# The Nyquist bin of a spectral attention block, with tokens on partitions and with new orders on all engines

## The reference

```python
query = unit_projection(x @ Wq.T + bq)      # F(x)/(|F(x)|+eps), back
keys, values = unit_projection(...), unit_projection(...)
s = jnp.cumsum(bind(keys, values), axis=1)  # along tokens
out = unbind(s, query)
x = x + out
x = x + ffn(layernorm(x))   # 8 trees of depth 7, 255 nodes: silu(logits) of the path's nodes @ W_out.T
```

## Time and profile before

| | |
|---|---|
| median of 3 runs | 1993.65 us |
| profiled execution | 1992.84 us |
| its span, first to last instruction | 1991.0 us |
| mean granted TensorE clock | 0.987 |
| TensorE busy | 1868.4 us (94%) |
| VectorE busy | 1744.3 us (88%) |
| ScalarE busy | 1131.1 us (57%) |
| POOL busy | 945.9 us (48%) |

### The profile page before, as it was taken

How to read it: one execution, slowest core, us unless ns; L and a number is a source line. 1 busy time by engine, 2 the same in 40 slices (tenths; PEclk the granted TensorE clock), 3 DMA queues, 4 the chain that set the end, 5 groups by cost and what they waited for, 6 DMA issues and landing times.

```text
span 1991.0 us, 39541 instructions
## 1 busy us (share of the span) xinstructions
PE 1868.4 (94%) x14360; PEld 1362.3 (68%) x14360; DVE 1744.3 (88%) x2900; ACT 1131.1 (57%) x2150; POOL 945.9 (48%) x744
## 2 busy tenths in 40 slices
PE   8489999999999999999999999999999999999978
PEld 6367766677766667766667776667776666776655
DVE  4988899988899889899988889998889998889983
ACT  5565555566555566555556555556655555655533
POOL 1354454554444554445555445455444555544540
PEclk9699999999999999999999999999999999999998
DMA  8022232222232222223222223222223322222312
GB/s 272 11 75 76 74 95 74 74 84 74 74 95 91 67 79 76 78 84 95 65 83 84 74 74 95 74 74 90 69 74 95 93 65 79 79 76 83 85 54 64
DMA packets 181642, 163.05 MB, mean 82 GB/s; under 512 B 140146, under 2 KB 140658, under 8 KB 181618
## 3 DMA queue, kind: packets, MB, share of 16 engines
q1 hardware_dynamic: 163186, 95.35, 16.6%
q0 software_dynamic: 18432, 67.38, 10.9%
HBM read 95.58 MB, written 16.78 MB: 56 GB/s over the span
## 4 chain that ended last, share of the span: by engine, by line
DVE 57%; issue 16%; PE 9%; POOL 5%; ACT 4%; DMA 2%; DVEq 1%; SPq 1%; POOLq 0%; ACTq 0%
DVE arena L1186 9%; PE bank_l L507 7%; DVE sp_hat L1131 6%; DVE arena L1209 4%; DVE arena L1199 4%; DVE sp_den L1125 3%; DVE dec L1179 3%; DVE xn_pair L1088 2%; DVE sp_cum L1154 2%; DMA arena<-xn_pair 2%; DVE arena L1142 2%; DVE st L1056 2%; DVE sp_den L1123 2%; DVE arena L1145 2%; DVE arena L1110 2%
## 5 line engine op out<-in xcount | busy, mean ns | idle before, releaser
L507 PE MATMUL bank_l<-arena,win_mem 128*128 128x256 f16 x5376 | 625.7, 273 | 27.4 <-DMA arena<-xn_pair 27.4
L542 PE MATMUL bank_l<-wout_mem,arena 128*128 128x512 f16 x2688 | 590.8, 379 | 0.3 <-DVE arena L1186 0.3
L507 PEld LDWEIGHTS bank_l<-arena,win_mem 128*128 128x128 f16 x5376 | 522.0, 98 | 96.5 <-issue 19.1
L477 PE MATMUL bank_p<-arena,wf_hi 128*128 128x256 f16 x3072 | 508.5, 273 | 18.0 <-DMA arena<-xn_pair 9.9
L542 PEld LDWEIGHTS bank_l<-wout_mem,arena 128*128 128x128 f16 x2688 | 263.0, 98 | 304.0 <-DVE arena L1186 0.8
L477 PE MATMUL bank_p<-arena,wf_lo 128*128 128x256 f16 x1536 | 419.3, 273 | 0.0
L935 POOL TENSOR_TENSOR arena<-arena 128x512 f32<-128x512 f32 x96 | 121.7, 1268 | 617.7 <-ACT arena L697 617.7
L477 PEld LDWEIGHTS bank_p<-arena,wf_hi 128*128 128x128 f16 x3072 | 296.1, 98 | 65.1 <-ACT arena L688 16.7
L742 ACT ACTIVATE arena<-bank_l,bias_in,s_logit 128x256 f32<-128x256 f32 x448 | 225.8, 558 | 168.1 <-PE bank_l L517 167.7
L1186 DVE SCALAR_TENSOR_TENSOR arena<-arena,s_act 128x512 f16<-128x512 f32 (+1 forms) x256 | 252.5, 1006 | 39.6 <-ACT arena L752 39.5
L1179 DVE TENSOR_SCALAR dec<-bank_l,thr,off 128x256 bf16<-128x256 f32 x256 | 131.9, 527 | 64.5 <-PE bank_l L507 64.2
(11 more groups left out here) (180 smaller groups left out, 2722.3 us busy)
## 6 DMA issues: line engine op xcount, KB each, us to landing
arena<-in_x SPq DMA_DIRECT2D x32, 512.0 KB, 3.6
arena<-arena SPq DMA_DIRECT2D x32, 512.0 KB, 2.9
out<-arena SPq DMA_DIRECT2D x64, 256.0 KB, 2.1
wout_mem<-in_w_in_t SPq DMA_DIRECT2D x1, 3584.0 KB, 15.1
arena<-in_w_out_t SPq DMA_DIRECT2D x1, 3584.0 KB, 14.1
arena<-xn_pair SPq DMA_TRANSPOSE x128, 2.7
arena<-in_leaf_rows,leaf_row POOLq DMA_INDIRECT x128, 4.9
win_mem<-in_wq SPq DMA_DIRECT2D x1, 1024.0 KB, 8.3
```

Source lines behind the costliest of these rows:

```text
L477: mm = pe.matmul(bank, a, b, start=(n == 0), stop=(n == len(pairs) - 1))
L507: mm = pe.matmul(bank_l[t % 4][:, c * T:(c + 1) * T], a[:, k, w:w + P], x2t[:, :, b, k, :], start=(c == 0 and k == 0 and m == 0), stop=((t ...
L542: mm = pe.matmul(bank_l[j][:, :], a[:, m, tok], w[:, m, :], start=(m == 0 and a is a_hi and w is wout_hi), stop=(m == DENSE - 1 and a is a ...
```

## The change

The Nyquist values of q, k and v leave the rows for token partitions. `nyquist_rows` turns `sp_raw` (96 partitions by 128 tokens) by two float32 products of 3 columns, into unused columns of `bank_i[1]`. ScalarE takes the size of 6 columns there (`nyquist_size`). VectorE works on 6 columns (`nyquist_den`, `nyquist_inverse`, `nyquist_unit`) and 2 columns (`nyquist_bind`). The running sum along the tokens is five float32 products with an upper triangle and a full square of one value (`nyquist_sums`). `nyquist_unbind` adds the carry and multiplies with q, and `nyquist_carry` makes the next carry. The inverse transform loses its one-row products. Instead the residual adds the value where it folds, with a sign by position. For that the stored order of the features puts odd positions ahead of even ones, and the two cosine folds become four of half the width.

The core of the diff:

```diff
+            def nyquist_rows(n):
+                pe.wait_ge(raw_im, 3 * n + 3)
+                if not isinstance(n, int) or n:
+                    pe.wait_ge(x1_ready, J * n)
+                for j in range(J):
+                    mm = pe.matmul(sp_rows[:, j, :], sp_raw[:, j * P:(j + 1) * P], row_of, start=True, stop=True)
+                mm.then_inc(sp_rows_full, 1)
+            def nyquist_sums(n):
+                pe.wait_ge(sp_kv_ready, n + 1)
+                pe.matmul(sp_sums[:, 0:1], upper, sp_kv[:, 0:1], start=True, stop=True)
+                pe.matmul(sp_sums[:, 1:2], upper, sp_kv[:, 1:2], start=True, stop=False)
+                pe.matmul(sp_sums[:, 1:2], full, sp_kv[:, 0:1], start=False, stop=True)
+                pe.matmul(sp_sums[:, 2:3], full, sp_kv[:, 0:1], start=True, stop=False)
+                pe.matmul(sp_sums[:, 2:3], full, sp_kv[:, 1:2], start=False, stop=True).then_inc(sp_sums_full, 1)
...
-                    if c == 0:
-                        pairs += [(sp_z_hi[:, tok], tab_sp[:, :]), (sp_z_lo[:, tok], tab_sp[:, :])]
...
-                act.activation(sp_den[:, :], sp_raw[:, :], ACT.Abs).then_inc(sp_abs_ready, 1)
+            def nyquist_size(n):
+                act.wait_ge(sp_rows_full, n + 1)
+                act.activation(sp_size, sp_rows, ACT.Abs).then_inc(sp_abs_ready, 1)
...
+            def nyquist_den(n):
+                dve.wait_ge(sp_abs_ready, n + 1)
+                dve.tensor_tensor(sp_den[:, :, :], sp_size, eps_sp[:, :, :], ALU.add).then_inc(sp_den_ready, 1)
+            def nyquist_inverse(n):
+                dve.wait_ge(sp_den_ready, n + 1)
+                dve.reciprocal(sp_den[:, :, :], sp_den[:, :, :]).then_inc(sp_inv_ready, 1)
+            def nyquist_unit(n):
+                dve.wait_ge(sp_inv_ready, n + 1)
+                dve.tensor_tensor(sp_hat[:, :, :], sp_rows, sp_den[:, :, :], ALU.mult).then_inc(sp_hat_ready, 1)
+            def nyquist_bind(n):
+                dve.wait_ge(sp_hat_ready, n + 1)
+                dve.tensor_tensor(sp_kv[:, :], sp_hat[:, :, K], sp_hat[:, :, V], ALU.mult).then_inc(sp_kv_ready, 1)
+            def nyquist_unbind(n):
+                dve.wait_ge(sp_sums_full, n + 1)
+                dve.scalar_tensor_tensor(out=sp_z[:, :], in0=sp_sums[:, 0:J], scalar=sp_carry[:, 0:1],
+                                         in1=sp_hat[:, :, Q], op0=ALU.add, op1=ALU.mult).then_inc(sp_z_ready, 1)
...
-                dve.tensor_tensor(cos[:, 0:QI], ce[:, 0:QI], co[:, 0:QI], ALU.add)
-                dve.tensor_tensor(cos[:, QI:], ce[:, 0:QI], co[:, 0:QI], ALU.subtract)
+                dve.wait_ge(sp_z_ready, i + 1)
+                top, odds, evens = sp_z[:, j:j + 1], slice(0, ODDS), slice(ODDS, QI)
+                for part, sign in ((odds, ALU.subtract), (evens, ALU.add)):
+                    up, down = cos[:, part], cos[:, QI + part.start:QI + part.stop]
+                    dve.scalar_tensor_tensor(out=up, in0=ce[:, part], scalar=top, in1=co[:, part], op0=sign, op1=ALU.add)
+                    dve.scalar_tensor_tensor(out=down, in0=ce[:, part], scalar=top, in1=co[:, part], op0=sign,
+                                             op1=ALU.subtract)
```

The orders of the engines in `step`. On ScalarE, after the copies of the odd parts:

```diff
+                act.activation(root_warm[:, :], ln_eps[:, :], ACT.Sqrt)
                 if attn:
                     evac_re(n, Q)
                     evac_im(n, Q)
                     square(n, Q)
+                std(i, mv2, rs2, ln2_mv, ln2_std)
+                if attn:
                     evac_re(n, K)
-                std(i, mv2, rs2, ln2_mv, ln2_std)
-                if attn:
-                    root(n, Q)
...
                     evac_im(n, K)
+                    root(n, Q)
                     square(n, K)
                     evac_re(n, V)
-                    root(n, K)
                     evac_im(n, V)
                     square(n, V)
...
+                    root(n, K)
                     root(n, V)
```

The silus move ahead of the high parts for trees 4 and 5, and `z_high` comes behind the first `leaf_silu`. On POOL:

```diff
                     sum_squares(n, K)
-                    q_unit(n)
                     sum_squares(n, V)
                     add_eps(n, K)
+                    q_unit(n)
+                fetch(i, 1)
+                if attn:
                     bind(n)
                 fetch(i, 0)
                 if attn:
                     unbind(n)
-                fetch(i, 1)
```

More of the change, by code:

```diff
@@ L623, in step @@
[L623 to L637 removed]
+                logits(i, 0, 0)
@@ L1505, in constants @@
     fwd[P, P:HB] = 0.0
[L1506 removed]
+    inside, even, odd = INSIDE, k[:P], k[P:]
     def angles(f, m):
```

309 lines of the change are left out of this document (155 added, 154 removed).

## The result

| | before | changed |
|---|---|---|
| median, 4 runs each | 1992.68 us | 1973.22 us |
| lowest to highest | 1987.29 to 1995.52 | 1970.82 to 1974.94 |
| ratio, 95% interval | | 0.9905 (0.988 to 0.9929) |
| profiled execution, its span | 1992.84, 1991.0 | 1974.17, 1972.3 |

The kernel is faster by 19.5 us, about 1%. The forecast was 47 us. So the direction and the range held, and more than half of the expected gain is missing.

A forecast was written before the change was run, and what follows sets the result against it. TensorE was taken to set the 59.15 us period: minus 2.94 stalls, minus 0.62, plus 1.8, plus 0.4 stall left gives 57.8. That saves 42 us over 31 periods, 47 with the ends: 1946 us, range 1928 to 1978.

The forecast's parts named there:

- (a): TensorE: removing two one-row products per half saves 0.31 us per half, 0.62 us per block.
- (d): TensorE: seven added float32 products with 1 to 3 columns, plus a shape change, cost 1.8 us per block, bounds 1.5 to 3.2.
- (f): Next block's split: both low halves come right after the first leaf dots, so the 0.43 us stall before the projections goes.
- (g): ScalarE at the seam: roots reordered and the residual starting at about 0 remove the 0.53 and 0.16 us stalls.
- (h): POOL fetches the second tree's rows before the binding products; the chain to the inverse transform keeps some 4 us of cover.
- (b): VectorE: long one-row products, combination, reciprocal, scan and smaller operations go, about 11 us per block.
- (c): VectorE: added operations on 6 or 2 columns and extra residual instructions cost 1.5 us per block.
- (e): Path counts moved further behind their trees: the 0.81 and 0.21 us stalls go if VectorE is at most about 1 us behind.
- The rule weighed: Whether POOL's multiplying holds small VectorE operations: all held, about 3 us instead of 0.8; only two-SBUF-input ones held, forecast stands.
- rival B: Middle stays stalled: small operations wait for POOL, tree 5 and 6 decisions over 1 us late; 1977 us, chance 0.2.
- C: Slower: the seven float32 products on TensorE don't overlap, 4.0 + 0.4 us instead of 1.8; 2027 us, chance 0.08.
- D: No gain: the float32 products on TensorE cost their upper bound of 3.2 us; 1989 us, chance 0.05.

The follow-up runs named there:

- e13: e11 with ScalarE's order at the block's seam (copy of K's real part, roots for q and k) as before the change: 1917.46 us, ratio 0.9633.
- e7: The kernel before the change with the Nyquist bin left out of the attention's output, all orders kept: 1958.00 us, ratio 0.9813.
- e11: e8 with the low part of tree 2 also moved behind the decision on tree 6: 1916.33 us, ratio 0.9611.
- e12: The changed kernel with one edit: POOL waits for its own previous product between its four binding products; 1916.53 us, ratio 0.9627.
- e2: The changed kernel with the next block's norm shift (reciprocal and `nb`) moved behind the decision on tree 6: 1935.22 us, ratio 0.9717.
- e3: The changed kernel with `nb` in place but made by two one-column operations with one SBUF tensor input each: 1934.16 us, ratio 0.9711.
- e10: e11 with the five float32 sum products of each block issued twice: 1954.23 us, ratio 0.98.
- e6: e2 with the norm shift put back in its old place, behind tree 4's low part and ahead of tree 7's decision: 1967.93 us, ratio 0.9881.
- e8: e2 with the combination `sp_kv` made by two one-column operations with a single SBUF tensor input each: 1934.04 us, ratio 0.9695.

## Why the prediction was wrong

By its own steps:

- **(a), (d), TensorE's work.** Right in kind, too dear in size. The seven products take 0.36 + 1.04 = 1.40 us and not 1.8; the change to the 96-row shape, for which I had 0.2 to 0.3, doesn't show. The period without stall is 56.8 us where I had 57.4. Where the other 0.2 us of the difference lies was not taken apart.
- **(f), (g), the seam.** Right: the 0.43, 0.53 and 0.16 us stalls are gone, and the residual starts with the projections. Why they went was only half right. In e13 the order of the roots that I argued with is worth nothing, and in e7 taking VectorE's Nyquist work away left most of the old stalls, which I had put down to it. That the seam came out as forecast is in this part luck.
- **(h) and the prologue.** Right: the inverse transform waits for nothing in the loop. The first one stands at 89.68 us where it stood at 91.69, 2.0 of the forecast 3 us. With the last block some 3 of the forecast 5 us outside the periods came.
- **(b), (c), VectorE's work.** The long one-row operations went, but busy time fell by 84 us and not by 300: `nb` takes 133 us in all where 30 times 1.03 us are 31, and the 128 leaf dots, L1233, take 1616 ns each where they took 680, 120 us more. They run beside POOL's sums and low parts, which follow the unbinding (in the block read the dots stand from 1019.15 to 1027.06, POOL's sums from 1018.76 and its low parts from 1023.79). With these two 84 + 102 + 120 = 306 us of work did go. Only the first of them costs time on TensorE's path: in e11 the leaf dots are as long (median 1631 ns) and TensorE waits for nothing in the loop.
- **(e) and "I leave 0.4 us of stall": the step that failed.** The stall is 1.9 us in the block read and 1.8 on average (58.60 - 56.81). One count waits 1.42 us, over the 1 us that I had named as a sign of being wrong. (e) said that the stalls go if VectorE is at most about 1 us behind at trees 5 and 6. It is, but for one thing: the diff moves `nb` to just ahead of the decision on tree 4, and I had put no price on it. The order of the instructions showed it there, beside the four Nyquist operations that I did price. e12 shows its price by one edit that leaves the place and the work alone, e2, e3 and e11 by others. The bill: 1.4 us more stall than forecast is 1.4 x 31 = 43 us slower, 0.6 us less work is 19 us faster, and 2 us outside the periods did not come: together about 27 us, the distance from 1946 to 1973.
- **The rule weighed.** I read the earlier trace rows as a hold of about one POOL instruction, 1 us, and rival B as 3 us for many of them. The rule itself stood up. The Trainium skill (SBUF — State Buffer, Who interferes with whom) says that a VectorE instruction with at most one SBUF input, outside the two-port modes, does not contend with GpSimd, and that one with two contends with a GpSimd instruction that reads SBUF. The traces agree: in e2, inside one chain of POOL, 150, 191 and 163 ns against 3609, and in e3, at the place of `nb`, 209 against 4438. Of VectorE's two-port modes the section says that whoever issues first gets the shared ports for the whole instruction. If that held for two inputs from SBUF too, `nb` would wait for one product of POOL, by my estimate at most 1.28 us. The measurement differs: 4.77 us, over four instructions of POOL.
- **The rivals.** B was nearest: VectorE late by over 1 us in the middle, 1977 us forecast, 1973 measured. Its place was half right (it named trees 5 and 6, the late ones are 4 and 5), and its cause was too broad: the "small operations" that it priced, the Nyquist ones, took 0.15 to 0.19 us in the block read, and `nb` was not among them. That its time came out so near is in part luck: B added 1.0 us of stall to the forecast, the run had 1.4 us more stall and 0.6 us less work. C and D, the expensive products, are ruled out by e10: 0.24 us each, where C needed 0.43.

One thing is left open. In the unbinding `nb` gets in at the first product's end (e6, and the kernel before), although POOL's rows overlap by 0.04 us there as in the binding. The product that it meets there lasts 1.69 us instead of 1.27, and it starts while a low part with two inputs from SBUF is still at work on VectorE (e6: low part 1009.98 + 0.72, product 1010.13), so it was most likely held first itself. The changed kernel shows the same in its unbinding: the first three products average 1.69 to 1.70 us, where the four of the binding average 1.26 to 1.28, and a low part of VectorE that starts at 1013.58 us in the first of them (1012.41 + 1.69 = 1014.10) lasts 1.07 us, to 1014.65, so it did not wait for the chain's end. Whether a product that was itself held is what lets VectorE in at the next boundary was not tried.

## What to carry to other kernels

Before a VectorE operation is moved, look at what POOL does at the new place, and count the tensor inputs from SBUF: a tiny operation with two of them can last as long as POOL's whole chain, and all decisions behind it wait. Cheap cures are scalar operands in place of a second tensor, a place behind the urgent operations, or a gap in POOL's chain; when one operation is freed, look for the next in line (here there were three). And when an engine looks overloaded, take its work away once in a run: here it gave 0.8 to 1.0 us of period and left most of the stall.

## What the runs showed of the hardware

- A VectorE operation on 128x2 with two SBUF tensor inputs lasted 4.4 us on average under four back-to-back POOL products of 1.27 us, and 1.09 us when POOL waited for its own product between them. The start-to-start step of POOL's products rose only from 1.23 to 1.36 us.
- The hold wanders: `nb` 4.4 us, then `sp_kv` 3.6 (e2), then the low part of tree 2, 2.5 for 0.74 us (e8).
- POOL's indirect DMA instruction did not hold VectorE in the block read. In the changed kernel one runs from 1006.50 for 0.98 us and the next from 1007.78 for 1.20. `sp_kv` starts at 1007.35 in the first and takes 0.16 us, and the low part at 1007.43, with two tensor inputs, reaches into the second and takes 0.75, its length when POOL is idle.
- Small float32 products in a dense stream step at 0.14 us for the first and 0.22 for the next, with 1 or 3 columns, and at 0.18 for 96 rows. Their records say 0.28 to 0.36 us. Doubling five of them cost 0.24 us each (e10).
